# Gathers one group further over the stage borders, and the order of loads, in a two-layer graph network kernel

## The reference, cut to what matters

```
xn = layernorm(x)
x = x + graph0(xn) + mix0(xn)       # graph0: segment sums of xn[src] and edge features by dst, one matmul, relu
x = x + experts0(layernorm(x))      # top 2 of 8 experts, silu(a) * b
xn = layernorm(x)
x = x + graph1(xn) + mix1(xn)       # graph1: weighted segment sum; mix1: linear attention, then feed forward, 2 norms
z = layernorm(x)
x = x + (layernorm(z + experts1(z)) * gamma + beta)     # top 2 of 16 experts, relu
```

## Time and profile before

| | |
|---|---|
| median of 3 runs | 2258.12 us (2255.16 to 2262.03) |
| the profiled execution | 2264.34 us, its span 2262.6 us |
| busy: TensorE, VectorE, ScalarE, Pool | 1907.8, 1248.4, 603.2, 1068.4 us |
| mean granted TensorE clock | 0.927 of full speed |
| DMA | 258.49 MB, mean 114 GB/s |

### The profile page before, as it was taken

The page is one execution under the profiler, slowest core; times in us unless marked ns, Lnnn a source line. Parts: engine busy times, 40 slices in busy tenths (PEclk is TensorE's granted clock), DMA queues, the critical chain, the costliest instruction groups (busy, mean ns, idle before and its releaser), DMA issues. The chain is left out here.

```text
span 2262.6 us, 33217 instructions
## 1 busy us (share of the span) xinstructions
PE 1907.8 (84%) x10298; PEld 1561.5 (69%) x10299; DVE 1248.4 (55%) x3125; ACT 603.2 (27%) x1303; POOL 1068.4 (47%) x1063
## 2 busy tenths in 40 slices
PE   6599788888576899999984989799999766799976
PEld 4366566666363799999982667578877653688865
DVE  7533687777475444444448568525544386233446
ACT  0222343333342111111113211122222132233324
POOL 0576777777520222222220667777777200355532
PEclk9999899999886899999996999899999987899998
DMA  7554555555364011011005533434444408212224
GB/s 228 152 147 130 151 145 144 141 140 148 88 274 170 28 35 34 30 35 34 30 22 165 177 102 113 115 116 131 124 127 116 138 1 355 80 63 65 67 62 145
DMA packets 175992, 258.49 MB, mean 114 GB/s; under 512 B 74113, under 2 KB 139357, under 8 KB 173460
## 3 DMA queue, kind: packets, MB, share of 16 engines
q0 software_dynamic: 49344, 131.89, 20.2%
q1 hardware_dynamic: 114644, 113.45, 15.2%
q10 hardware_dynamic: 11904, 11.96, 1.6%
HBM read 203.27 MB, written 56.86 MB: 115 GB/s over the span
## 5 line engine op out<-in xcount | busy, mean ns | idle before, releaser
L575 POOL DMA_INDIRECT agg_message<-table,edges_src x784 | 790.5, 1008 | 397.7 <-issue 233.7
L630 PE MATMUL agg_partial<-agg_message,moe_up 128*128 128x321 f32 x784 | 243.3, 465 | 71.2 <-DMA agg_message<-table,edges_src 58.6
L2463 PEld LDWEIGHTS ex_p_h<-ex_xT,ex_own_up 128*128 128x128 f32 (+1 forms) x2464 | 280.0, 191 | 2.8 <-issue 1.4
L2463 PE MATMUL ex_p_h<-ex_xT,ex_own_up 128*128 128x128 f32 (+1 forms) x2464 | 280.7, 276 | 1.0 <-DVE ex_xT L2514 1.0
L630 PEld LDWEIGHTS agg_partial<-agg_message,moe_up 128*128 128x128 f32 x784 | 158.5, 205 | 147.5 <-issue 86.0
L630 PE MATMUL agg_partial<-agg_message,agg_onehot 128*128 128x256 f32 x784 | 188.4, 394 | 19.4 <-DMA agg_message<-table,edges_src 10.4
L2422 POOL DMA_INDIRECT ex_x<-moe_in,route_token_at x58 | 57.3, 987 | 309.8 <-PE ex_p_x L2453 240.7
L2518 DVE COPY ex_own_up<-moe_up 128x1280 f32 x114 | 100.7, 884 | 167.2 <-PE ex_p_h L2463 166.4
L630 PEld LDWEIGHTS agg_partial<-agg_message,agg_onehot 128*128 128x128 f32 x784 | 153.6, 198 | 48.4 <-issue 25.1
L640 ACT COPY agg_span<-agg_partial 128x321 f32<-128x321 f32 (+1 forms) x112 | 44.9, 401 | 435.4 <-PE agg_partial L633 426.5
L2588 POOL DMA_INDIRECT ex_x<-moe_in,route_token_at x66 | 64.4, 975 | 172.9 <-PE ex_p_x L2619 93.1
(11 more groups left out here) (588 smaller groups left out, 3318.3 us busy)
## 6 DMA issues: line engine op xcount, KB each, us to landing
agg_message<-table,edges_src POOLq DMA_INDIRECT x784, 2.8
agg_message<-in_edge_rows SPq DMA_DIRECT2D x56, 224.0 KB, 4.3
moe_up<-in_f_w SPq DMA_DIRECT2D x8, 1386.0 KB, 21.7
sums<-agg_span SPq DMA_DIRECT2D x56, 160.5 KB
moe_up<-in_f_w SPq DMA_DIRECT2D x4, 2048.0 KB
moe_down<-in_f_w SPq DMA_DIRECT2D x4, 2048.0 KB, 32.7
sums<-agg_span SPq DMA_DIRECT2D x56, 128.0 KB
moe0b_down<-in_f_w SPq DMA_DIRECT2D x8, 768.0 KB, 10.5
```

Source lines behind the costliest of these rows:

```text
L575: pool.indirect_dma_start(out=to[:, k * w:k * w + D], out_offset=None, in_=self.table, in_offset=bass.IndirectOffsetOnAxis(ap=self.edges.s ...
L630: mm = pe.matmul(to, hot[:, k * P:(k + 1) * P], msg[:, k * w:(k + 1) * w], start=(k == 0), stop=(g == 0 and k == GE - 1))
L2463: return pe.matmul(to, own_up[:, o:o + n], xT[:, k * D + c * P:k * D + (c + 1) * P], start=(c == 0), stop=(c == 1))
```

## The change

The constant `AHEAD` is 2. At the borders within a layer Pool gathers one group more before the border and one less behind it; the number of gathers stays. In `keys_and_values` the first group's loads come as tiles 0 and 1, with a semaphore of their own, and tiles 2 to 4; VectorE's loop takes them as two pieces. In `finish` SyncE issues the ten loads, half by half, and ScalarE none; ScalarE makes both groups of `shares(2, .)` before those of `shares(1, .)`. In the routing of layer 1, SyncE issues the first two `up` loads at the start of its program, ahead of the stores, the other six behind them as before.

```diff
@@ qkv_channels, gpsimd
-            for g in range(groups[0] + 1, groups[-1] + 2):
+            for g in range(groups[0] + 1, groups[-1] + AHEAD + 1):
@@ mixer, gpsimd
-            for g in range(groups[0] + 1, EG):
+            for g in range(groups[0] + AHEAD, EG):
@@ keys_and_values
+    FIRST = 2
...
+        first_loaded = m.sem("first_loaded")
...
             if g >= 3:
                 eng.wait_ge(taken, g - 2)
-            first = s * NPAD + g * GT * P
-            eng.dma_start(got[g % 3][:, s * GT * D:(s + 1) * GT * D].rearrange("p (i d) -> p i d", d=D),
-                          rows[first:first + GT * P, :].rearrange("(i p) d -> p i d", p=P)).then_inc(loaded[g % 3], 16)
+            if g == 0:
+                part(eng, s, 0, FIRST, first_loaded)
+                part(eng, s, FIRST, GT, loaded[0])
+            else:
+                part(eng, s, g * GT, (g + 1) * GT, loaded[g % 3])
+
+        def part(eng, s, a, b, landed):
+
+            to = got[a // GT % 3][:, (s * GT + a % GT) * D:(s * GT + a % GT + b - a) * D]
+            eng.dma_start(to.rearrange("p (i d) -> p i d", d=D),
+                          rows[s * NPAD + a * P:s * NPAD + b * P, :].rearrange("(i p) d -> p i d", p=P)).then_inc(landed, 16)
...
-            for e in range(0, groups[-1] + 2):
+            for e in range(0, groups[-1] + AHEAD + 1):
...
-                if n == 0 and s == 0:
+                if i == 0 and s == 0:
+                    dve.wait_ge(first_loaded, 32)
+                elif s == 0 and (i == FIRST or g and n == 0):
                     dve.wait_ge(loaded[g % 3], (g // 3 + 1) * 32)
...
-            for g in range(2):
-                for i in range(g * GT, (g + 1) * GT):
+            for a, b in ((0, FIRST), (FIRST, GT), (GT, 2 * GT)):
+                for i in range(a, b):
                     add(i, 0)
-                if g:
+                if a == GT:
                     scales(0)
                 c.settle()
-                for i in range(g * GT, (g + 1) * GT):
+                for i in range(a, b):
                     add(i, 1)
                 c.settle()
-                for i in range(g * GT, (g + 1) * GT):
+                for i in range(a, b):
                     measure(i)
-                if g == 0:
+                if b == GT:
                     spreads(0)
@@ attend, gpsimd
-            for e in range(groups[0] + 1, groups[-1] + 2):
+            for e in range(groups[0] + AHEAD, groups[-1] + AHEAD + 1):
@@ feed_forward, gpsimd
-            for e in range(groups[0] + 1, EG):
+            for e in range(groups[0] + AHEAD, EG):
@@ Routing.build, sync
+            for to, of, landed in ahead:
+                sp.dma_start(to, of).then_inc(landed, 16)
             for g in range(NG):
                 sp.wait_ge(tile_ready, (g + 1) * GT)
@@ finish, sync
-            load(sp, 0, 0)
+            for k in range(2):
+                load(sp, 0, k)
             sp.dma_start(beta_row[:, :], row(beta)).then_inc(beta_loaded, 16)
             for g in range(1, NG):
-                load(sp, g, 0)
+                for k in range(2):
+                    load(sp, g, k)
             sp.dma_start(gamma_row[:, :], row(gamma)).then_inc(gamma_loaded, 16)
@@ finish, scalar
-            act.wait_ge(cleared, 64)
-            for g in range(NG):
-                load(act, g, 1)
             for g in range(2):
                 shares(2, g)
+            for g in range(2):
                 shares(1, g)
@@ build
-                              [(to, of, up_loaded) for to, of in up_parts] + [(to, of, down_loaded) for to, of in down_parts])
+                              ahead=[(to, of, up_loaded) for to, of in up_parts[:2]],
+                              behind=[(to, of, up_loaded) for to, of in up_parts[2:]]
+                              + [(to, of, down_loaded) for to, of in down_parts])
```

More of the change, by code:

```diff
@@ L29 @@
 RING = 3
+AHEAD = 2
 QKV_GROUPS = 15
@@ L2073, in __init__, with route @@
         self.loaded = m.sem("loaded")
-    def route(self, nc, const, X, w, bias, table, measured=None, behind=()):
+    def route(self, nc, const, X, w, bias, table, measured=None, ahead=(), behind=()):
         with ExitStack() as ctx:
-            self.build(nc, Memory(nc, ctx, f"{self.tag}r"), ctx, const, X, w, bias, table, measured, behind)
+            self.build(nc, Memory(nc, ctx, f"{self.tag}r"), ctx, const, X, w, bias, table, measured, ahead, behind)
     def gates(self, dve, c, asked, exped, biased):
@@ L2110, in exponentials, with build @@
         act.activation(self.second[:, :], self.second[:, :], ACT.Exp).then_inc(exped, 1)
-    def build(self, nc, m, ctx, const, X, w_in, bias, table, measured, behind):
+    def build(self, nc, m, ctx, const, X, w_in, bias, table, measured, ahead, behind):
         ne, tj = self.ne, self.tiles
```

## The result

The changed kernel takes 2251.82 us in the median of 8 runs (2246.56 to 2257.10), the kernel before 2259.34 us on the same chip. The ratio is 0.9964, 95% interval 0.9953 to 0.9975: 8.1 us faster, where 24.3 us were forecast. 2251.8 us lies outside my range of 2226 to 2247.

The account below looks back on a forecast made before the run. Pool's indirect gathers were taken to bound layer 0's mixer stage, chains of other engines much of the rest. Terms -8.8 - 10.3 - 2.0 - 3.7 + 0.5 = -24.3 us off the 2258.12 us median gave 2233.8 us, range 2226 to 2247.

Parts of the forecast that it names:

- layer 0's border: Border before layer 0's mixer stage: Pool starts one group further behind it, so the stage ends 8.8 us sooner (7.0 to 9.24).
- layer 1's borders: Three borders up to feed forward: 3.0 us lost before attend, later waits shortened, together -10.3 us (-6.5 to -11.5).
- first rows in two pieces: Keys and values, layer 1: VectorE starts on two tiles while the rest land, 2.0 us sooner (-0.5 to -2.1).
- last loads by SyncE: Last stage: ScalarE, freed of its loads, makes shares sooner; VectorE then waits for gamma; -3.7 us (0 to -8.5).
- half of up weights ahead: Layer 1's routing: loading sooner gains 0, the router's weights may land late; +0.5 us (0 to +3.3).
- Pool bounds the stage to its end: Layer 0's mixer stage: Pool issues gathers without pause, so the whole 8.8 us lead reaches the stage's end.
- the forecast of 0.7 us more from later waits: Later in layer 1's feed forward: four waits on gathers, 5.5 us in all, give up to 1.4 us, taken as 0.7.
- The wait of 4.5 us for gamma: Last stage, a sign of being right: VectorE's first gamma product waits some 4.5 us for a DMA.
- Gamma lands with its turn: Rival, 12%: the one queue hands gamma over by 2216, the last stage gives 8.5 us; 2229 us.
- The borders give less: Rival, 18%: layer 1 gives 6.5 us and the router's weights are 3 us late; 2240 us.
- Only layer 0 pays: Rival, 4%: only the 8.8 us of layer 0 come, as layer 1's gather is hidden anyway; 2249 us.
- Slower: Rival, 3%: gathers themselves stretch, to a mean of 1.07 us in place of 1.008; 2265 us.

## Why the prediction was wrong

The range missed by one term. The table sets each term against what the profiles of the first comparison and of the last two chips show, as the mean of those with the part less the mean of those without it (us):

```
term                               forecast   measured   profiles with / without
layer 0's border                     -8.8       -6.5      6 / 3, start of the graph stage
layer 1's borders                   -10.3       -7.6      4 / 3, keys' start to neighbour rows' start, less the pieces
first rows in two pieces             -2.0       -1.9      keys' start to the first gather of layer 1
last loads by SyncE                  -3.7       -2.6      last stage's start to the first centering
half of up weights ahead             +0.5      +10.6      routing's start to the logits
sum                                 -24.3       -8.0      measured as a whole: -8.1
```

A slip in the prediction's bounds: the best ones together are 9.24 + 11.5 + 2.1 + 8.5 = 31.3 us, not 31.6. The range would have begun at 2226.8, and nothing hangs on it.

**The step that failed: half of the up weights ahead, +0.5 with bounds 0 to +3.3.** I looked at the stores' cover and at the router's weights, and priced these by 128 KB rows that landed in 7.2 to 8.8 us. The weights did land in 7.5 us, inside those bounds. The bias row behind them on ScalarE's queue landed in 13.5, and I had left it out, since VectorE adds it only much later; but TensorE's program begins with a wait for both. I had asked who uses the weights first, and not what TensorE's first wait counts. In its place the runs show +10.6 us, nearly all of it ahead of TensorE's first turn (13.9 us into the stage, not 3.6). The gain of 0 was right: with the loads kept but behind the router's rows the time is level with none ahead. No run has TensorE wait for the weights alone; by their landing it would still have started 3.8 us late (an estimate: 1853.4 less 1846.0, less 3.6).

The Trainium skill (DMA: Bandwidth & Descriptors, "Queues, rings and completion order") has an engine take turns between queues packet by packet, from which I had drawn a delay of a few turns. The trace agrees with the turns, but they are not few. These are the packets of the changed kernel from 1845.9 to 1853.5, until the weights landed, and those of the two small loads in the kernel before, 1861.5 to 1866 (queue, packets, MB, share of the time of 16 engines):

```profile
q1 hardware_dynamic: 175, 2.61, 87.7%
q10 hardware_dynamic: 159, 0.02, 1.6%
```

```profile
q10 hardware_dynamic: 288, 0.02, 4.0%
```

q10 is ScalarE's queue, q1 SyncE's. The two small loads make 288 packets, 18 for each of the 16 engines, and beside the large loads nearly each of them waits for one of SyncE's: 159 against 175. A large packet takes 0.61 us (an estimate: 87.7% of 16 engines over 7.6 us, by 175). So 18 turns are 11 us for both loads, and half of that for the weights; measured are 10.9 us more for the bias row (13.5 in place of 2.6) and 5.9 for the weights (7.5 in place of 1.6). My sum by the row of the small loads was nearer than a few turns, and still too low.

**Layer 0, right in its mechanism, too large by some 2.3 us.** The border did what was forecast: group 17 starts 8.6 us sooner on the mean (230.1 to 231.1 against 238.9 to 239.4). "Pool bounds the stage to its end" is the sentence that failed. With the lead, Pool meets the slot of group 18 still in use and waits 3.2 to 3.6 us in five of six profiles (1.35 in the sixth); without it, 0.3 to 1.64 us. At group 22 the lead is 6.4 us (277.3 to 280.0 against 285.0 to 285.6), and the profile with the short wait has the largest, 8.0. The ends of the stage spread more (610.1 to 617.4 us with the further group, 618.9 to 622.0 without), so the 6.5 of the table is less firm than the 6.4. I had read the 2.1 us of slot waits of the earlier trace rows as a property of the stage, when it was one of Pool's lateness. That this wait is the cause is read from the profiles, not shown by an experiment: a fourth slot was not tried.

**Layer 1, right up to the feed-forward, then too large.** The keys' border costs 3.3 us (forecast 3.0). Attend and the first turn give what was said: TensorE's first turn in feed forward moved by 11.6 us within the layer (284.8 to 273.2 us behind its start, means), without the pieces 9.7, where I took 9.6. The step that failed is the forecast of 0.7 us more from later waits: the rest of the stage takes 314.1 us without the further group and 316.2 with it. Pool is on the path in its second half: products 43 to 45, 51 and 52 each start as soon as their gathers are in, 1.9 us behind the issue of the last one (before, 45 and 52 alone). I had counted the waits as what is left to gain; they were the sign of the engine that bounds. This too is read from profiles, and no run tests it.

**Last stage, 1.1 us short, for another reason than said.** The first base product came 0.47 us behind the stage's start, as forecast. VectorE began on the means 18.5 us into it; with 0.95 us for them, as before, it would have been ready at 19.5, where I had 17.6, as its last statistics come later than I moved them. Gamma landed 8.1 us after its issue, at 23.5 us and not at 22.4. And VectorE's own chain was ready at nearly that moment, being held by Pool's additions. The wait of 4.5 us for gamma is one of the signs that I had named, and it shows as 0.33 us; moving gamma alone gave nothing, moving both rows and Pool's start gave 3. That one queue is as fast as two held: the last of the experts' rows landed 23.2 us into the stage, 22.9 before.

**The rivals.** "Gamma lands with its turn" fell. "The borders give less" was the right direction for the borders (14.1 us together, forecast 19.1) and its router term of 3 was the right place at a third of its size. "Only layer 0 pays" fell with the 7.6 us of layer 1, and "Slower" fell: mean gathers 1.007 us against 1.008. The chance of 93% for faster held; the range failed because its worst case had one unpriced load in it.

## What to carry to other kernels

Before a large transfer is moved ahead, list every small load on every queue that is issued in the same few microseconds, and for each the first wait that counts it, not the first operation that reads it. Price it by its packets, each with one packet of the large load ahead of it, and not by its bytes; issuing the small rows first, and the large ones once they have landed, keeps both. A lead of one more buffer is worth what the ring can hold: the next wait is for the slot, and it does not show in a profile in which the producer is late. And a free engine's large operation is not free if it holds another engine's small ones; start it where that one is waiting anyway.

## What the runs showed of the hardware

- A load of 8 KB behind one of 16 KB on ScalarE's queue took 13.5 us beside 2 x 2 MB on SyncE's, and 2.6 us beside nothing. The packets of the two queues went nearly one for one (159 against 175 until the 16 KB had landed), and a large one took some 0.61 us. The 4.2 MB were through at about the same moment, but the 16 KB landed at 1853.4, with 2.6 MB moved: they did not wait for the whole.
- VectorE's operations of 128x10 or 128x128 elements took up to as long as one of Pool's additions (2.9 us) beside them: 2.93 and 2.23 us for what takes 0.17 else, up to 2.97 us for a share that takes 0.27 else. Its statistics of 128x256, at 0.43 us, did not stretch. The Trainium skill (SBUF — State Buffer, "Who interferes with whom") describes an exclusive lock on the ports that these two engines share, held for the whole instruction, which the ends at 2215.67 and 2215.70 bear out.
- The granted clock of TensorE was 0.53 in a product behind 6.91 us without work, and 1.00 in the same product behind 0.55 us; the product took 6.13 and 3.26 us.
- Two speeds of chip: 2259 and 2262 us, or 2482 and 2488, with a mean granted clock of TensorE of 0.924 to 0.935 and 0.895 to 0.907 over the spans of the profiled executions. The excess lies where gathers and products run together; why is open. The further group at layer 0's border gave 0.9937 there and 0.9966 here, with intervals that overlap.
